# First block of a state-space and attention kernel: one exponential moved to ScalarE, key blocks placed elsewhere around the taps, input loads reordered

## The chip, the cores and the metric

The kernel runs on one NeuronCore of a Trainium2 chip. The metric is the device time of one execution in microseconds (us). The program is one launch made of several blocks that end in a barrier of all engines; the change touches the first of them only.

## The reference, cut to what matters

Two adaLN-like layers act on x (64 sequences of 32 tokens, 512 wide): a convolution along the feature axis with kernels that a state-space model gives, then a feed-forward layer with low-rank experts, then attention over a paged cache of keys and values, then a second feed-forward layer. The first block of the kernel computes the convolution, and beside it turns the cached keys for the attention.

```python
dt = jnp.exp(log_dt)
A = -jnp.exp(log_A_real) + 1j * A_imag
dtA = A * dt[:, None]
P = dtA[:, :, None] * jnp.arange(length, dtype=jnp.float32)
Cs = Cc * (jnp.exp(dtA) - 1.0) / A
K = 2.0 * jnp.einsum('hn,hnl->hl', Cs, jnp.exp(P)).real      # (32 heads, 512 taps)
...
k_f = jnp.fft.rfft(kernel, n=n); u_f = jnp.fft.rfft(u_m, n=n)
y = jnp.fft.irfft(u_f * k_f, n=n)[..., :Lq]                  # causal convolution per head
y = y + u_m * D[:, None]
return y * mask[:, None, :]
...
x = x + L0_ffn(L0_cond(x, ...), ...)
x = x + L1_ffn(L1_cond(x, ..., k_cache, v_cache, ...), ...)
```

## The kernel before

The first block is the function `prologue`. Its work, by engine:

- **VectorE** computes dt and A from 32-column tiles, then the angles (48 multiples of the imaginary part of dtA for each of 2048 modes, a 128x768 tile), brings them into the range of the sine (`reduce_angle`), then computes the magnitudes: `exp_exact` is an exponential out of 14 VectorE operations on the 128x768 tile (clamp, split off the power of two, a polynomial). It multiplies magnitude by sine and cosine (`er`, `ei`), works out the coefficients (sums of products in 128x16 tiles), and hands `ur`, `ui` over. Every operation waits for the one before it (class `Line`). Later it makes the masks, adds D to the taps, reduces the angles of the rotary embedding (128x1024 tiles), and then masks the result of each of the 32 heads (L312).
- **ScalarE** takes the sines of angles (L348), copies turned keys from PSUM to SBUF (`lay_out(n)`, L336, two operations for a block), copies half of the taps (L352), writes the taps to a DRAM scratch `taps` (L354), and reads them back as a Toeplitz tile for each head (`load(h)`, L342, tile `s_toe`, six buffers). These six buffers mean that head h+6 is loaded when head h is through.
- **TensorE** turns blocks of cached keys by transposes (`turn(n)`, L378: eight 128x128 transposes for a block, 16 blocks in all), computes the taps (L390: 128 small matmuls), and then convolves: four matmuls for each of the 32 heads (L399), which read the reversed input `um` and `s_toe`.
- **SyncE** loads the small inputs and the key blocks (`k_in`, four buffers, 512 KB a block), stores the turned blocks (`k_t`, L203), and loads the first feed-forward layer's weights after the store of block 12. The block can end only when all 16 stores have landed (L210).
- **GpSimd** multiplies the rotary tables; it isn't late for anything in this block.

Three things set the order of the key blocks. `EARLY = 9` blocks are turned before the taps. The others follow a head each: `late(h)` gives block 9 after head 3, block 10 after head 7, and so on to block 15 after head 27. And block n+4 is loaded when the copies of block n are done.

There are two DMA queues in use here: SyncE's (queue 1 in the profile) and ScalarE's (queue 10). Before the change the four loads of `um`, 1 MB each, stand in ScalarE's queue.

Of the kernel before, what the change touches and what calls it, by code (L numbers as in the profile page):

```python
# [19 lines left out]
ALU = mybir.AluOpType  # L20
ACT = mybir.ActivationFunctionType
AX = mybir.AxisListType

P = 128
# [29 lines left out]
NMUL = 48  # L54
# [46 lines left out]
def spread(ap, axis, n):  # L101

    ap = ap.unsqueeze(axis)
    shape = list(ap.shape)
    shape[axis] = n
    return ap.to_broadcast(shape)
# [35 lines left out]
def prologue(nc, ps, dram, taps, cst, um, mrow, k_t, y_t, cos, sin, ta, tb, inputs):  # L142
# [6 lines left out]

    TB, YB, EARLY, H = 4, 4, 9, D // 2  # L150
    TOE = 6
    with ExitStack() as ctx:
# [29 lines left out]
        flat = lambda x: x.rearrange("p a b -> p (a b)")  # L182
        late = lambda h: EARLY + h // 4 if h % 4 == 3 and EARLY + h // 4 < KT else None

        with nc.Block() as block:
            @block.sync
            def _(e):
                src = bass.AP(tensor=dram["L0_cond_log_dt"].tensor, offset=0, ap=[[0, P], [1, S]])
                e.dma_start(log_dt[:, :], src).then_inc(s_dt, 16)
                e.dma_start(raw[:, 1, :], dram["log_a"]).then_inc(s_dt, 16)  # L190
                e.dma_start(ai[:, :], dram["a_imag"]).then_inc(s_in, 16)
                e.dma_start(cc[:, :, :], dram["c"]).then_inc(s_in, 16)
                e.dma_start(dvec[:, :], dram["L0_cond_D"].rearrange("(o h) -> o h", o=1)).then_inc(s_in, 16)

                def load(n):
                    e.dma_start(k_in[:, n % TB, :], dram["k_cache"][n * P:(n + 1) * P, :]).then_inc(s_ki[n % TB], 16)

                for n in range(TB):
                    load(n)
                k_rows = k_t.rearrange("(t n d) x -> t d n x", n=PPT, d=P)  # L200
                for n in range(KT):
# [26 lines left out]
            def _(e):  # L228
# [18 lines left out]
                mulb = spread(mul, 1, HP)  # L247
                e.wait_ge(s_cst, 16)
                v(lambda e: e.tensor_tensor(ang[:, :, :], spread(dai, 2, NMUL), mulb, ALU.mult))
                reduce_angle(v, flat(ang[:, :, :]), flat(t1[:, :, :]), flat(sn[:, :, :]), flat(cs[:, :, :]))  # L250
                done["angles"] = line.n
                v(lambda e: e.tensor_tensor(ang[:, :, :], spread(dar, 2, NMUL), mulb, ALU.mult))
                exp_exact(v, flat(ang[:, :, :]), flat(mag[:, :, :]), flat(t1[:, :, :]), flat(t2[:, :, :]), flat(t3[:, :, :]))
                e.wait_ge(s_sin, 2)
                v(lambda e: e.tensor_tensor(er[:, :, :], mag[:, :, :], cs[:, :, :], ALU.mult))
                v(lambda e: e.tensor_tensor(ei[:, :, :], mag[:, :, :], sn[:, :, :], ALU.mult))

                zr, zi, nr, ni, x, u = w[3], ei[:, :, 1], w[4], w[5], w[6], w[7]
                cr, ci = cc[:, :, 0], cc[:, :, 1]
# [6 lines left out]
                v(lambda e: e.tensor_tensor(ni, ni, x, ALU.add))  # L266
                sr, si, den = w[8], w[9], w[10]
                v(lambda e: e.tensor_tensor(sr, nr, ar, ALU.mult))
# [4 lines left out]
                v(lambda e: e.tensor_tensor(si, si, x, ALU.subtract))  # L273
                v(lambda e: e.tensor_tensor(den, ar, ar, ALU.mult))
                v(lambda e: e.tensor_tensor(x, ai[:, :], ai[:, :], ALU.mult))
                v(lambda e: e.tensor_tensor(den, den, x, ALU.add))
                v(lambda e: e.reciprocal(u, den))
                v(lambda e: e.scalar_tensor_tensor(out=sr, in0=sr, scalar=2.0, in1=u, op0=ALU.mult, op1=ALU.mult))
# [38 lines left out]
            def _(e):  # L317
# [4 lines left out]
                for kind, name in enumerate(("L1_cond_q_norm_w", "L1_cond_k_norm_w")):  # L322
                    row = bass.AP(tensor=dram[name].tensor, offset=0, ap=[[0, P], [1, D]])
                    e.dma_start(nw[:, kind, :], row).then_inc(s_len, 16)
                for k in range(KB):
                    e.dma_start(um[:, k, :, :], dram["x_rev"][k * P:(k + 1) * P, :, :]).then_inc(s_x, 16)
                e.wait_ge(s_v, done["zeros"])
# [12 lines left out]
                def load(h):  # L340
                    src = bass.AP(tensor=taps.tensor, offset=h * KPW + 1, ap=[[1, P], [1, L]])
                    e.dma_start(toe[:, h % TOE, :], src).then_inc(s_toe[h % TOE], 16)  # L342

                for n in range(2):
                    lay_out(n)
# [3 lines left out]
                for n in range(2, EARLY):  # L349
# [4 lines left out]
                e.dma_start(taps[:, P:KPW].rearrange("h (a b) -> a h b", b=32),  # L354
                            kev[:, :, :, :].rearrange("a i t b -> a (i t) b")).then_inc(s_out, 16)
                e.wait_ge(s_out, 32)
                for h in range(TOE):
                    load(h)
                e.wait_ge(s_v, done["rope"])
                for x in (sin, cos):  # L360
# [9 lines left out]
            def _(e):  # L370
# [15 lines left out]
                for i in range(HP):  # L386
                    for a, b, first in ((ur, er, True), (ui, ei, False)):
                        for half in range(2):
                            rows = slice(half * NS, (half + 1) * NS)
                            last = e.matmul(ps[0:16, half, i * 32:(i + 1) * 32], a[rows, i, :], b[rows, i, 0:32],  # L390
                                            start=first, stop=not first)
                            if i == HP - 1 and not first:
                                last.then_inc(s_k, 1)
                e.wait_ge(s_x, 16 * KB)
                for h in range(S):
# [1250 lines left out]
```

## Time and profile before

| | |
|---|---|
| median of 3 runs | 2441.7 us (2440.74 to 2443.94) |
| the profiled execution's own time | 2454.87 us |
| its span, first to last instruction | 2453.0 us |
| TensorE busy | 2400.6 us, 98% of the span |
| VectorE, ScalarE, GpSimd busy | 1878.4, 1310.2, 719.9 us |
| the first block | 0 to about 98.8 us of the span |

The profiled execution is 13.2 us longer than the median of the runs; it serves to find where time goes, and differences are what is carried from it to the runs. Busy shares are means over the whole span, and the first block is 4% of it, so the first block is read by its own timeline.

### The profile page before, as it was taken

To read this page: it belongs to the slowest core of one execution; us is meant where nothing else is said; L and a number is where in the kernel's file an instruction comes from. 1 tells how busy PE (TensorE), PEld (TensorE's weight loads), DVE (VectorE), ACT (ScalarE), POOL (GpSimd) and SP (SyncE) were. 2 spreads that over 40 slices of the span, in tenths; PEclk is the share of its full clock that TensorE was granted. 3 is DMA by queue.
4 is the path that set the end of the run, shared out by engine and by line. 5 is a ranking of instruction groups with operands and counts; after the bars stand their busy time and mean duration, and the time that the engine had idled before them with its cause. 6 is when DMAs were issued, how large, how long until landed. Compare 5 with 4: busy or idle time off the path is not lost. (4 is left out here: it accounts for less than half of the span.)

```text
span 2453.0 us, 53992 instructions
## 1 busy us (share of the span) xinstructions
PE 2400.6 (98%) x16104; PEld 2167.1 (88%) x16104; DVE 1878.4 (77%) x3317; ACT 1310.2 (53%) x3758; POOL 719.9 (29%) x712
## 2 busy tenths in 40 slices
PE   5999999999999999999999999999999999999999
PEld 4888777777777999999999999999999998888877
DVE  7559999999961887788778877788778876666653
ACT  2335555555543677677767776676667761111120
POOL 1206666666641122222222222222222213131100
PEclk9999999999999999999999999999999999999999
DMA  8732333333347688888888888888788879666622
GB/s 312 258 120 87 94 98 95 95 115 94 98 125 245 222 295 276 294 298 291 281 285 303 295 284 282 293 297 295 273 295 295 295 268 283 219 209 207 204 69 103
DMA packets 434117, 542.36 MB, mean 221 GB/s; under 512 B 36980, under 2 KB 350100, under 8 KB 429460
## 3 DMA queue, kind: packets, MB, share of 16 engines
q1 hardware_dynamic: 390724, 394.24, 48.7%
q0 software_dynamic: 36864, 134.23, 16.2%
q10 hardware_dynamic: 6480, 13.26, 1.5%
q8 instruction: 28, 0.46, 0.1%
q14 instruction: 21, 0.17, 0.0%
HBM read 440.59 MB, written 101.01 MB: 221 GB/s over the span
## 5 line engine op out<-in xcount | busy, mean ns | idle before, releaser
L1296 DVE CUSTOM_DVE_ANT_0 at_sm<-ps,at_mask 128x544 f32<-128x544 f32 x512 | 369.3, 721 | 256.2 <-PE ps L1209 247.7
L1242 PE MATMUL ps<-at_pt,at_v_raw 128*128 128x128 f32 x4096 | 540.9, 275 | 1.7 <-issue 1.7
L1242 PEld LDWEIGHTS ps<-at_pt,at_v_raw 128*128 128x128 f32 x4096 | 497.6, 192 | 1.9 <-issue 1.9
L1359 ACT ACTIVATE at_pt<-ps 128x512 f32<-128x512 f32 x512 | 303.9, 594 | 299.4 <-PE ps L1218 194.9
L942 POOL TENSOR_TENSOR pr_m<-pr_qn,tb 128x256 f32<-128x256 f32 x320 | 331.6, 1056 | 307.0 <-DVE pr_qn L911 291.8
L1372 ACT ACTIVATE at_pr<-at_sm,at_nm 128x544 f32<-128x544 f32 x512 | 383.1, 748 | 59.1 <-DVE at_nm L1296 54.9
L1289 DVE TENSOR_TENSOR at_k_lo<-shared,at_k_hi 128x1088 fp32r<-128x1088 f32 x256 | 325.9, 1273 | 0.0
L762 PE MATMUL ps<-pr_hi,xh 128*128 (+1 forms) x768 | 317.7, 414 | 6.1 <-DVE pr_qn L911 5.0
L1167 POOL DMA_INDIRECT at_v_raw<-v_cache,at_idx x256 | 276.9, 1082 | 113.9 <-issue 62.0
L1218 PE MATMUL ps<-constants,at_pr 128*128 128x128 f32 x2048 | 306.5, 272 | 0.0
L764 PE MATMUL ps<-pr_hi,xl 128*128 (+1 forms) x768 | 303.3, 395 | 0.0
L763 PE MATMUL ps<-pr_lo,xh 128*128 (+1 forms) x768 | 303.2, 395 | 0.0
L868 ACT ACTIVATE pr_sq<-ps 128x128 f32<-128x128 f32 x640 | 168.0, 277 | 229.7 <-DVE f_a L904 224.4
L1173 POOL COPY at_idx<-at_rows 128x4 uint32 (+1 forms) x64 | 11.8, 184 | 868.4 <-PE ps L1249 801.7
L1209 PE MATMUL ps<-at_k_hi,at_q_hi 128*128 128x272 f32 x1024 | 255.5, 330 | 3.1 <-issue 1.2
L1218 PEld LDWEIGHTS ps<-constants,at_pr 128*128 128x128 f32 x2048 | 243.5, 140 | 0.0
L1209 PE MATMUL ps<-at_k_hi,at_q_lo 128*128 128x272 f32 x1024 | 211.9, 288 | 0.0
L1209 PE MATMUL ps<-at_k_lo,at_q_hi 128*128 128x272 f32 x1024 | 211.2, 287 | 0.0
L1477 ACT ACTIVATE op_ohi<-o_raw 128x2048 fp32r<-128x2048 f32 x31 | 59.6, 1922 | 273.5 <-PE ps L1534 243.1
L1530 PE MATMUL ps<-op_ohi,op_wlo 128*128 128x512 f32 x512 | 201.2, 393 | 0.0
L1529 PE MATMUL ps<-op_ohi,op_whi 128*128 128x512 f32 x512 | 200.9, 392 | 0.0
L922 DVE TENSOR_TENSOR pr_m<-pr_qn,ta 128x512 f32<-128x512 f32 x160 | 195.9, 1224 | 0.0
(239 smaller groups left out, 4299.3 us busy)
## 6 DMA issues: line engine op xcount, KB each, us to landing
shared<-k_t SPq DMA_DIRECT2D x1024, 128.0 KB
qk_t<-pr_stage SPq DMA_DIRECT2D x160, 256.0 KB, 2.3
shared<-qk_t SPq DMA_DIRECT2D x64, 512.0 KB, 7.3
o_t<-at_ot SPq DMA_DIRECT2D x64, 512.0 KB
shared<-ri_d SPq DMA_DIRECT2D x32, 1024.0 KB, 8.3
o_raw<-o_t SPq DMA_DIRECT2D x32, 1024.0 KB, 6.1
f_w<-wqkv SPq DMA_DIRECT2D x12, 1024.0 KB, 5.9
s_k_in<-k_cache SPq DMA_DIRECT2D x16, 512.0 KB, 8.0
```

Source lines behind the costliest of these rows:

```text
L762: e.matmul(out, xh[:, k, cols], hi, start=(k == 0), stop=False)
L763: e.matmul(out, xh[:, k, cols], lo, start=False, stop=False)
L764: last = e.matmul(out, xl[:, k, cols], hi, start=False, stop=(k == KB - 1))
L942: ins = e.tensor_tensor(heads(m2[:, q, :])[:, :, a], heads(qn[:, q, :])[:, :, b], table(tb, i, j - 3, a), ALU.mult)
L1167: e.indirect_dma_start(out=v_raw[:, q, c, :], out_offset=None, in_=dram["v_cache"], in_offset=bass.IndirectOffsetOnAxis(ap=idx[:, q, c:c + ...
L1209: last = e.matmul(ps[:, 2 * r + h, 0:W], a[:, q, mine], b[:, w, g % 2, h * W:(h + 1) * W], start=first, stop=end)
L1218: last = e.transpose(ps_w(jj % 2)[:, c * P:(c + 1) * P], pr[:, w, k, c * P:(c + 1) * P], ident)
L1242: e.matmul(sums(w, k), v_raw[:, q, c, g * D:(g + 1) * D], pt[:, jj % 4, c * P:(c + 1) * P], start=(k == 0 and c == 0), stop=False, skip_gr ...
L1289: e.tensor_tensor(two(k_lo), raw, two(k_hi).bitcast(F32), ALU.subtract).then_inc(s_lo, 1)
L1296: e.tensor_tensor_reduce(out=halves(sm[:, r, :]), in0=ps[:, 2 * r:2 * r + 2, 0:W], in1=halves(mask[:, q, :]), scale=-SC, scalar=3e38, op0= ...
L1359: e.activation(pt[:, jj % 4, :], ps_w(jj % 2), ACT.Copy).then_inc(s_pt, 1)
L1372: e.activation(pr[:, w, k, :], sm[:, r, :], ACT.Exp, bias=nm[:, at], scale=-1.0, accum_out=su[:, at]).then_inc(s_e, 1)
```

## The change

The diff, with all that concerns the steps:

```diff
-    TB, YB, EARLY, H = 4, 4, 9, D // 2
+    TB, YB, EARLY, GAP, H = 4, 4, 5, 8, D // 2
...
-        late = lambda h: EARLY + h // 4 if h % 4 == 3 and EARLY + h // 4 < KT else None
+        late = lambda h: GAP + h // 4 if h % 4 == 1 and GAP + h // 4 < KT else None
...
                 e.dma_start(raw[:, 1, :], dram["log_a"]).then_inc(s_dt, 16)
+
+                def load(n):
+                    e.dma_start(k_in[:, n % TB, :], dram["k_cache"][n * P:(n + 1) * P, :]).then_inc(s_ki[n % TB], 16)
+
+                load(0)
                 e.dma_start(ai[:, :], dram["a_imag"]).then_inc(s_in, 16)
                 e.dma_start(cc[:, :, :], dram["c"]).then_inc(s_in, 16)
                 e.dma_start(dvec[:, :], dram["L0_cond_D"].rearrange("(o h) -> o h", o=1)).then_inc(s_in, 16)
...
-                for n in range(TB):
+                for n in range(1, TB):
                     load(n)
+                for k in range(KB):
+                    e.dma_start(um[:, k, :, :], dram["x_rev"][k * P:(k + 1) * P, :, :]).then_inc(s_x, 16)
...
                 e.wait_ge(s_cst, 16)
+                v(lambda e: e.tensor_tensor(t2[:, :, :], spread(dar, 2, NMUL), mulb, ALU.mult))
+                done["exponents"] = line.n
                 v(lambda e: e.tensor_tensor(ang[:, :, :], spread(dai, 2, NMUL), mulb, ALU.mult))
                 reduce_angle(v, flat(ang[:, :, :]), flat(t1[:, :, :]), flat(sn[:, :, :]), flat(cs[:, :, :]))
                 done["angles"] = line.n
-                v(lambda e: e.tensor_tensor(ang[:, :, :], spread(dar, 2, NMUL), mulb, ALU.mult))
-                exp_exact(v, flat(ang[:, :, :]), flat(mag[:, :, :]), flat(t1[:, :, :]), flat(t2[:, :, :]), flat(t3[:, :, :]))
-                e.wait_ge(s_sin, 2)
...
+                v(lambda e: e.tensor_tensor(den, ar, ar, ALU.mult))
+                v(lambda e: e.tensor_tensor(x, ai[:, :], ai[:, :], ALU.mult))
+                v(lambda e: e.tensor_tensor(den, den, x, ALU.add))
+                v(lambda e: e.reciprocal(u, den))
+                e.wait_ge(s_sin, 3)
...
-                for k in range(KB):
-                    e.dma_start(um[:, k, :, :], dram["x_rev"][k * P:(k + 1) * P, :, :]).then_inc(s_x, 16)
...
+                e.wait_ge(s_v, done["exponents"])
+                e.activation(mag[:, :, :], t2[:, :, :], ACT.Exp).then_inc(s_sin, 1)
                 for n in range(2):
                     lay_out(n)
...
                             kev[:, :, :, :].rearrange("a i t b -> a (i t) b")).then_inc(s_out, 16)
+                for n in range(EARLY, EARLY + 2):
+                    lay_out(n)
                 e.wait_ge(s_out, 32)
                 for h in range(TOE):
                     load(h)
+                for n in range(EARLY + 2, GAP):
+                    lay_out(n)
...
+                for n in range(EARLY, GAP):
+                    turn(n)
                 e.wait_ge(s_x, 16 * KB)
```

The four operations on `den` and `u` are the same as before and stand earlier. After it, blocks 0 to 4 are turned ahead of the taps, 5 to 7 between the taps and head 0, and 8 to 15 behind heads 1, 5, ..., 29.

On ScalarE, from its first DMA on, this stands in order before (L336 is the copy of turned keys, L348 the sines, L352 and L354 the taps, L361 the rotary sines):

```order
L328 DMA taps<-s_zeros 32x128
L336 ACT_TABLE_LOAD
L336 ACTIVATE s_k_out<-ps 128x4x4x32 x4
L348 ACT_TABLE_LOAD
L348 ACTIVATE s_sn<-s_sn 128x768
L348 ACTIVATE s_cs<-s_cs 128x768
L336 ACTIVATE s_k_out<-ps 128x4x4x32 x14
L352 ACTIVATE s_kev<-ps 16x16x32
L354 DMA taps<-s_kev 16x32x32
L342 DMA s_toe<-taps 128x512 x6
L361 ACTIVATE shared<-shared 128x1024 x2
```

And this now:

```order
L346 ACT_TABLE_LOAD
L346 ACTIVATE s_mag<-s_t 128x768
L337 ACTIVATE s_k_out<-ps 128x4x4x32 x4
L351 ACT_TABLE_LOAD
L351 ACTIVATE s_sn<-s_sn 128x768
L351 ACTIVATE s_cs<-s_cs 128x768
L337 ACTIVATE s_k_out<-ps 128x4x4x32 x6
L355 ACTIVATE s_kev<-ps 16x16x32
L357 DMA taps<-s_kev 16x32x32
L337 ACTIVATE s_k_out<-ps 128x4x4x32 x4
L343 DMA s_toe<-taps 128x512 x6
L337 ACTIVATE s_k_out<-ps 128x4x4x32 x2
```

The exponential (`s_mag`) stands first, the number of table loads in this stretch is two in both, and of the 14 copies that stood between the sines and the taps six are left; four stand between the write of the taps and the first reads, two behind these.

On SyncE's queue the start was this:

```order
L190 DMA s_raw<-log_a 128x16
L191 DMA s_ai<-a_imag 128x16
L192 DMA s_cc<-c 128x32
L193 DMA s_dvec<-L_cond_D 1x32
L196 DMA s_k_in<-k_cache 128x1024 x4
L203 DMA k_t<-s_k_out 128x4x256
```

And it is this now:

```order
L190 DMA s_raw<-log_a 128x16
L193 DMA s_k_in<-k_cache 128x1024
L196 DMA s_ai<-a_imag 128x16
L197 DMA s_cc<-c 128x32
L198 DMA s_dvec<-L_cond_D 1x32
L193 DMA s_k_in<-k_cache 128x1024 x3
L202 DMA um<-x_rev 128x2048 x4
L206 DMA k_t<-s_k_out 128x4x256
```

The first key block has passed three small inputs, and the 4 MB of `um` stand ahead of the first store and of key block 4.

On TensorE, the rows behind the last matmul of the taps (L397) are these now; before, the row of 24 transposes (three blocks) was part of the 72 at the start, and after head 0 came heads 1 to 3 before a block:

```order
L397 MATMUL ps<-s_ei,s_ui 16x32 x2
L385 MATMUL ps<-constants,s_k_in 128x128 x24
L408 MATMUL ps<-um,s_toe 128x256
L408 MATMUL ps<-um,s_toe 128x192
L408 MATMUL ps<-um,s_toe 128x128
L408 MATMUL ps<-um,s_toe 128x64
```

There is one key block more among the heads than before (eight instead of seven), and three between taps and heads.

## Rows read from the trace of the kernel before

**Rows 1.** The page: span, and busy time of each engine.
```profile
span 2453.0 us, 53992 instructions
PE 2400.6 (98%) x16104; PEld 2167.1 (88%) x16104; DVE 1878.4 (77%) x3317; ACT 1310.2 (53%) x3758; POOL 719.9 (29%) x712
```

**Rows 2.** Waits of 0 to 200 us: total, times, longest.
```profile
PE ps L399 <- DMA s_toe<-taps: 8.6, 1, 8.6
```

**Rows 3.** Timeline of VectorE in the first block: start, length (us), line, operation.
```profile
9.27 0.17 DVE L246 TENSOR_TENSOR s_small<-s_ai,s_ex 128x16 f32<-128x16 f32 x1
...
18.41 0.56 DVE L111 TENSOR_SCALAR s_ang<-s_ang 128x768 f32<-128x768 f32 x1
...
30.32 0.96 DVE L255 TENSOR_TENSOR s_er<-s_mag,s_cs 128x768 f32<-128x768 f32 x1
...
35.05 0.17 DVE L274 TENSOR_TENSOR s_small<-s_small 128x16 f32<-128x16 f32 x1
...
35.97 0.18 DVE L278 SCALAR_TENSOR_TENSOR s_small<-s_small 128x16 f32<-128x16 f32 x1
...
98.19 0.59 DVE L312 TENSOR_TENSOR shared<-ps,mrow 128x256 f32<-128x256 f32 x1 [0.60 <-PE ps L399]
```

**Rows 4.** Timeline of ScalarE (ACT) and its DMA queue (ACTq).
```profile
19.54 0.85 ACT L348 ACTIVATE s_sn<-s_sn 128x768 f32<-128x768 f32 x1
...
43.77 0.33 ACTq L354 DMA_DIRECT2D taps<-s_kev  x1
47.91 2.76 ACTq L342 DMA_DIRECT2D s_toe<-taps  x6
...
59.18 1.08 ACT L336 ACTIVATE s_k_out<-ps 128x512 f32<-128x512 f32 x2 [3.60 <-PE ps L378]
```

**Rows 5.** Timeline of TensorE; a row may merge many instructions.
```profile
33.97 1.97 PE L378 MATMUL ps<-constants,s_k_in 128*128 128x128 f32 x8 [0.74 <-DMA s_k_in<-k_cache]
...
39.17 0.29 PE L390 MATMUL ps<-s_er,s_ur 64*16 64x32 f32 x4
...
42.46 0.22 PE L390 MATMUL ps<-s_ei,s_ui 64*16 64x32 f32 x4
51.32 7.33 PE L399 MATMUL ps<-um,s_toe 128*128 128x256 f32 x32 [8.64 <-DMA s_toe<-taps]
...
92.32 1.04 PE L378 MATMUL ps<-constants,s_k_in 128*128 128x128 f32 x8
93.20 4.95 PE L399 MATMUL ps<-um,s_toe 128*128 128x256 f32 x32
99.10 1.49 PE L625 MATMUL ps<-shared,f_g 128*32 128x512 f32 x11 [0.95 <-PEq L185]
```

**Rows 6.** Stretches: busy time of each engine, granted clock, DMA share, GB/s.
```profile
0.00:40.00 40.00, 18.52 (x104) 14.95 (x106) 32.31 (x76) 14.67 (x22) 0.95 (x6) 1.00 0.91 352
46.00:56.00 10.00, 4.68 (x16) 4.36 (x17) 7.91 (x9) 2.00 (x2) 0.34 (x1) 0.50 0.63 187
60.00:80.00 20.00, 20.00 (x143) 19.28 (x142) 8.57 (x14) 3.52 (x7) 14.26 (x7) 1.00 0.99 340
80.00:99.00 19.00, 18.15 (x129) 17.34 (x127) 8.46 (x14) 3.25 (x6) 0.00 (x0) 1.00 0.93 321
```

**Rows 7.** DMA issues of 0 to 200 us: count, KB each, median us to landing.
```profile
s_k_in<-k_cache SPq DMA_DIRECT2D x16, 512.0 KB, 8.0
k_t<-s_k_out SPq DMA_DIRECT2D x16, 512.0 KB, 7.1
s_toe<-taps ACTq DMA_DIRECT2D x32, 256.0 KB, 5.5
um<-x_rev ACTq DMA_DIRECT2D x4, 1024.0 KB, 14.8
```

**Rows 8.** The same for block 13's store, issued at 82.86 us.
```profile
k_t<-s_k_out SPq DMA_DIRECT2D x1, 512.0 KB, 12.6
```

**Rows 9.** The same for block 15's store, issued at 94.1 us.
```profile
k_t<-s_k_out SPq DMA_DIRECT2D x1, 512.0 KB, 4.3
```

More of the change, by code:

```diff
@@ L193, in _ @@
                 e.dma_start(dvec[:, :], dram["L0_cond_D"].rearrange("(o h) -> o h", o=1)).then_inc(s_in, 16)
-                def load(n):
-                    e.dma_start(k_in[:, n % TB, :], dram["k_cache"][n * P:(n + 1) * P, :]).then_inc(s_ki[n % TB], 16)
-                for n in range(TB):
+                for n in range(1, TB):
                     load(n)
+                for k in range(KB):
+                    e.dma_start(um[:, k, :, :], dram["x_rev"][k * P:(k + 1) * P, :, :]).then_inc(s_x, 16)
                 k_rows = k_t.rearrange("(t n d) x -> t d n x", n=PPT, d=P)
@@ L251, in _ @@
                 done["angles"] = line.n
-                v(lambda e: e.tensor_tensor(ang[:, :, :], spread(dar, 2, NMUL), mulb, ALU.mult))
-                exp_exact(v, flat(ang[:, :, :]), flat(mag[:, :, :]), flat(t1[:, :, :]), flat(t2[:, :, :]), flat(t3[:, :, :]))
-                e.wait_ge(s_sin, 2)
+                zr, zi, nr, ni, x, u = w[3], ei[:, :, 1], w[4], w[5], w[6], w[7]
+                sr, si, den = w[8], w[9], w[10]
+                v(lambda e: e.tensor_tensor(den, ar, ar, ALU.mult))
[3 more added lines that the diff above has]
+                e.wait_ge(s_sin, 3)
                 v(lambda e: e.tensor_tensor(er[:, :, :], mag[:, :, :], cs[:, :, :], ALU.mult))
                 v(lambda e: e.tensor_tensor(ei[:, :, :], mag[:, :, :], sn[:, :, :], ALU.mult))
-                zr, zi, nr, ni, x, u = w[3], ei[:, :, 1], w[4], w[5], w[6], w[7]
                 cr, ci = cc[:, :, 0], cc[:, :, 1]
@@ L266, in _ @@
                 v(lambda e: e.tensor_tensor(ni, ni, x, ALU.add))
-                sr, si, den = w[8], w[9], w[10]
                 v(lambda e: e.tensor_tensor(sr, nr, ar, ALU.mult))
@@ L273, in _ @@
                 v(lambda e: e.tensor_tensor(si, si, x, ALU.subtract))
[L274 to L277, printed above, removed]
                 v(lambda e: e.scalar_tensor_tensor(out=sr, in0=sr, scalar=2.0, in1=u, op0=ALU.mult, op1=ALU.mult))
```

## The prediction

> **What bounds the kernel now.** The page comes first: TensorE is busy in 98% of the span [rows 1], so time can only be won where TensorE stands still or runs slowly, or where a whole block is shortened. All that is edited lies in the first block, which ends with VectorE's last mask at 98.19 + 0.59 = 98.8 us [rows 3]; TensorE starts the next block at 99.10 [rows 5]. I therefore read the first 100 us by timelines, engine by engine, and take the rest as moved in one piece: behind 99 us nothing is edited, and no engine there waits for something that is timed from the launch.
>
> The first block has two stages. Up to 51.3 us a chain runs: VectorE's angles and magnitudes, then `er` at 30.32, the coefficients, the taps on TensorE until 42.46 + 0.22 = 42.7 us, the write of the taps at 43.77, their reads from 47.91, head 0 at 51.32 [rows 3 to 5]. The one long wait of TensorE in it is the 8.6 us for the first Toeplitz tile [rows 2]. Until the taps are ready the key blocks only fill gaps. The second stage, 51.32 to 93.20 + 4.95 = 98.15 us, is TensorE's: 32 heads and seven key blocks back to back [rows 5].
>
> A third thing must be watched. The DMA engines move 352 GB/s on average over the first 40 us, and are at a share of 0.99 with 340 GB/s from 60 to 80 [rows 6]. Block 13's store took 12.6 us to land, with the feed-forward weights ahead of it [rows 8]. The block ends when the slowest of TensorE's and SyncE's strands ends, and the second is close: block 15's store landed at 94.1 + 4.3 = 98.4 [rows 9], 0.4 us before VectorE was done.
>
> **The change part by part.** *The exponential.* `exp_exact` held VectorE from 18.41 to 30.32, 11.9 us [rows 3]. Now `er` waits for the three ScalarE operations. The product of the exponents moves ahead of the angles, so the angles are ready at 18.4 instead of 17.4 (one 128x768 product is 0.96 long and starts 1.0 before the next). The two sines take 0.85 each less some overlap [rows 4]: 18.4 + 1.6 + 0.2 for the semaphore = 20.25. The exponential is the same shape, about 0.85, and lies under VectorE's angles; its cover is VectorE's angles, from about 10.5 (one product and its gap behind the 9.5 us at which they began [rows 3]) to 18.4. So `er` starts at 20.25 instead of 30.32: 10.1 us off. The four operations for the reciprocal took 35.97 - 35.05 = 0.9 us on the chain [rows 3]; now they run in the wait for the sines: 0.9 off. Sum: 11.0 us earlier at the taps, whose matmuls then start at 39.17 - 11.0 = 28.2 and end at 31.7 [rows 5].
>
> *Key block 0 ahead of three small inputs.* These come perhaps 1.5 us later, and VectorE uses the first of them at 9.27 [rows 3]. No row says how long they had been there. I take 0; the bound is 1.5 us late.
>
> *Blocks 5 to 8 leave the front, `um` goes to SyncE's queue.* TensorE needs five blocks before the taps, 2.0 us each [rows 5]. Block 4 is now behind three key blocks, 4 MB of `um` and one store in its queue: with the constants and itself 7.7 MB. At 352 GB/s, a mean that holds the slow start of the launch [rows 6], that is there at 22 us and turned at 24; TensorE is wanted at 28.2. So 0, with 4 us of slack.
>
> *Blocks 5 to 7 between taps and head 0.* They fill TensorE's 8.6 us hole. The taps are written at 43.77 - 11.0 = 32.8 and need 47.91 - 43.77 = 4.1 us, so ScalarE may read at 36.9. Before that it has four copies, 1.1 us a block [rows 4]; block 6 is turned by 31.7 + 4.0 = 35.7 at the slow pace and copied by 36.8: just in time. The first tile then needs 51.32 - 47.91 = 3.4 us if nothing is in its way. Before, SyncE's queue was idle then; now two or three pairs of a store and a load are in flight. The median landing over the block is 5.5 us [rows 7], so the surcharge lies between 0 and 2.1; I take 1.0. Head 0 starts at 36.9 + 3.4 + 1.0 = 41.3, **10.0 us earlier** (9.0 to 11.0).
>
> *The heads.* One more key block is 93.20 - 92.32 = **0.9 us more**. Before, the first four heads ran 7.33 against 4.95 us for the last four [rows 5]: the granted clock is 0.50 from 46 to 56 us, the 1.2 GHz level [rows 6]. It fell after TensorE had been still since 42.7. Now the last block is turned near 37 to 38 and TensorE is still for 3 to 4 us. So 0 to 2.4 us come back; I take the middle, **1.2 us less**. The last head ends at 41.3 + 46.8 + 0.9 - 1.2 = 87.8.
>
> A remark on that clock: the Trainium skill (TensorE: Matmul & The Clock Gate, part 1, the clock gate) says that the array's default is the throttled level, and that activity releases it. The page of the profile shows 1.00 over the first 40 us, yet eight transposes took 1.97 us there and 1.04 at 92 us; the durations side with the skill, so that the turns of the front run at the slow level in both kernels. By the granted clock alone blocks 5 to 7 would take half as long; head 0 would not come sooner, since the taps' 4.1 us end later than these.
>
> *The end of the block.* Block 15 was turned at 92.32, and its store landed at 98.4, 6.1 us later, with four heads (4.95 us) to cover it. Now only two heads, 2.5 us, stand behind it. The turn starts 0.9 + 2.5 = 3.4 us before the last head's end, at 84.4; the store lands at 90.5. The block ends there and not at 87.8 + 0.6 = 88.4: **2.1 us lost**.
>
> *The same end by DMA.* The block moves 16 x 0.52 MB in, the same out, 32 x 0.26 MB of Toeplitz tiles, 4.2 MB of `um` [rows 7], 0.4 of constants and 1.6 of weights: 31.4 MB. 14.1 are through at 40 us (352 GB/s); 17.3 more at 340 to 360 GB/s are 48 to 51 us: 88 to 91. Both ways agree, so DMA is no further loss, but it stands right behind.
>
> Sum: 98.8 becomes 90.5 to 90.6, a shift of 10.0 + 1.2 - 0.9 - 2.1 = 8.2. The profiled execution would be 2454.87 - 8.2 = 2446.7 (span 2444.8). The runs' median lies 13.2 under the profiled one; with it, **2441.7 - 8.2 = 2433.5 us**. A measurement tells about 0.2% (4.9 us) from nothing.
>
> **Rivals.** *A. The next block starts slowly.* TensorE would stand still from 87.8 to 90.9, 3 us. After 42.7 it was granted 1.00 for a while and 0.50 from 46 on. If DMA is the later strand (91) or the heads end early, the still time passes 3.3 us and the clock may fall. L625, 3.6 us at full pace, then takes 7.2: gain 4.7, 2437.0.
>
> *B. `um` holds up the taps.* Block 4 is turned after 28.2 if the 7.7 MB take more than 26.2 us, which is under 294 GB/s from the launch on. The Trainium skill (DMA: Bandwidth & Descriptors, Queues, rings and completion order) says that descriptors of one queue are taken in ring order; no load can pass `um` by it. At 259 GB/s the block lands at 29.7 and is turned at 31.7: 3.5 us late, gain 4.7, also 2437.0. For it: 352 GB/s is what two queues did together, and now nearly all is in one. Against it: even with its slow start the stretch was 20% above the limit.
>
> *C. All goes well.* No surcharge on the first tile, the clock stays up, and block 15 lands in 5.4: 1.0 + 1.2 + 0.7 more: gain 11.1, 2430.6.
>
> *D. The Toeplitz tiles starve: slower.* Six tiles are in flight, and head h+6 must land within about five heads and a block, 7.1 us. Landings had a median of 5.5. The stores and loads of blocks 5 to 11 now run beside them throughout. If landings went to 9.5 us, six heads would take 9.9, 1.65 each, 53 us for the 32 and with the key blocks 60 against 47: 13 lost, 8.2 + 0.3 won, 2446. It decides from a landing of about 8.6 on. For it speaks the share of 0.99 [rows 6]; against it, that 60 to 80 us were just such a stretch and TensorE was busy 20.00 of 20 us.
>
> *E. It doesn't shorten the chain*: ScalarE must copy blocks 0 and 1 before the sines. If key block 1 came only as late as before, the sines would stay at 19.54, only 1.1 us late; to cancel everything it would have to come 10 us later. Gain near 0 only with B in its worst form: 2441.
>
> **How the numbers follow.** Forecast (gain 6.5 to 10) 0.60; A 0.14; B 0.07; C 0.11; D 0.04; E 0.04. The range from C's 2430.6, with 0.6 to spare, to A's and B's 2437.0 with 0.5: 2430.0 to 2437.5. It holds the forecast's cases, and most of A, B and C. Faster by over 0.2% means a gain over 4.9: the forecast, C, and about half of A and B, and what scatters beyond: 0.85. Slower is D: 0.04. The same: 0.11.
>
> **What would show it.** In the profile after: `er` at 20 to 21 us; the taps' matmuls ended by 32; block 4's turn done before them and no wait of these on `k_in`; first read of the taps at 37, head 0 at 40.5 to 42; heads at 1.2 us each; last head's end at 86.5 to 89, the last `k_t` store landing 2 to 3 us behind it, and SyncE's wait for it as the one that ends last; the next block's TensorE at 91 with a granted clock of 1.00. It would be wrong if `er` waited for ScalarE, if TensorE waited for `s_toe` more than a few tenths after head 0, or if stores queued up and the block ended well behind 91.

## The result, and the profile after

The changed kernel took 2438.87 us (median of 20 runs, 2435.49 to 2442.88), the kernel before 2443.81 us (20 runs, 2440.74 to 2448.12). The ratio is 0.998, with a 95% interval of 0.9974 to 0.9986: 4.9 us faster (3.4 to 6.4), where 8.2 were forecast. The time lies 1.4 us above the forecast's range.

The page of the changed kernel: span, and busy time of each engine, which answers to [rows 1].

```profile
span 2436.9 us, 53979 instructions
PE 2386.3 (98%) x16104; PEld 2160.7 (89%) x16104; DVE 1876.4 (77%) x3303; ACT 1320.2 (54%) x3759; POOL 718.1 (29%) x712
```

The profiled execution of the kernel before, 2454.87 us, lies above all of its twenty runs here, that of the changed kernel, 2438.88, is one of its twenty. So I take it that the two profiles come from different chips, and chips differ: the kernel before had medians of 2443.8, 2460.9, 2455.4 and 2461.6 us on four of them. Therefore I compare the stages of the first block and not the spans. Profiles of the same kernel, two of the one before and three of the changed one, start the next block within 0.4 us of each other, and head 0 within 0.5 us (before) and 1.2 us (changed). The waits of 0 to 200 us, total, times, longest, beside [rows 2]:

```profile
PE ps L385 <- DMA s_k_in<-k_cache: 19.7, 3, 10.4
...
PE ps L408 <- DMA s_toe<-taps: 5.9, 1, 5.9
```

VectorE's timeline, beside [rows 3]:

```profile
6.67 0.37 DVE L240 COPY s_raw<-s_log_dt 64x16 f32<-64x16 f32 x2 [5.69 <-DMA s_raw<-log_a]
...
21.43 0.96 DVE L264 TENSOR_TENSOR s_er<-s_mag,s_cs 128x768 f32<-128x768 f32 x1 [0.80 <-ACT s_cs L351]
...
90.17 0.59 DVE L315 TENSOR_TENSOR shared<-ps,mrow 128x256 f32<-128x256 f32 x1 [0.60 <-PE ps L408]
```

`er` starts 8.9 us earlier than in [rows 3], and waits 0.8 us for the second sine, as forecast. But VectorE's first copy starts at 6.67, and before at 5.33: the whole chain begins 1.3 us late. ScalarE and its queue, beside [rows 4]:

```profile
34.04 0.33 ACTq L357 DMA_DIRECT2D taps<-s_kev  x1
34.47 2.06 ACT L337 ACTIVATE s_k_out<-ps 128x512 f32<-128x512 f32 x4 [0.86 <-PE ps L385]
37.03 3.37 ACTq L343 DMA_DIRECT2D s_toe<-taps  x6
```

TensorE, beside [rows 5]; 30 like rows of the taps' matmuls are left out:

```profile
26.25 1.97 PE L385 MATMUL ps<-constants,s_k_in 128*128 128x128 f32 x8 [10.43 <-DMA s_k_in<-k_cache]
29.36 0.29 PE L397 MATMUL ps<-s_er,s_ur 64*16 64x32 f32 x4 [1.14 <-DVE s_ui L291]
...
32.65 0.30 PE L397 MATMUL ps<-s_ei,s_ui 64*16 64x32 f32 x4
32.88 2.11 PE L385 MATMUL ps<-constants,s_k_in 128*128 128x128 f32 x16
35.71 1.06 PE L385 MATMUL ps<-constants,s_k_in 128*128 128x128 f32 x8 [0.71 <-ACT s_k_out L337]
42.64 4.66 PE L408 MATMUL ps<-um,s_toe 128*128 128x256 f32 x16 [5.87 <-DMA s_toe<-taps]
...
87.61 2.52 PE L408 MATMUL ps<-um,s_toe 128*128 128x256 f32 x16
91.98 3.64 PE L634 MATMUL ps<-shared,f_g 128*32 128x512 f32 x32 [1.85 <-PEq L185]
```

Head 0 starts at 42.64 (8.7 us earlier), the last head ends at 87.61 + 2.52 = 90.13, the next block starts at 91.98 (7.1 earlier). The 16 matmuls of heads 0 and 1 took 4.66 us, and those of heads 30 and 31 took 2.52. The stretches show why (busy time of PE, PEld, DVE, ACT, POOL, then the granted clock, the DMA share and GB/s), beside [rows 6]:

```profile
28.00:40.06 12.06, 6.92 (x154) 6.17 (x152) 10.01 (x21) 3.31 (x7) 0.00 (x0) 0.78 0.93 310
40.06:46.89 6.83, 4.25 (x14) 3.92 (x15) 4.22 (x6) 3.09 (x4) 0.95 (x1) 0.50 0.99 341
46.89:60.00 13.11, 13.11 (x96) 12.65 (x96) 5.52 (x9) 3.05 (x6) 13.11 (x7) 1.00 1.06 401
60.00:80.00 20.00, 20.00 (x143) 19.28 (x142) 8.51 (x15) 3.47 (x7) 4.53 (x2) 1.00 1.03 360
```

TensorE had been still since 35.71 + 1.06 = 36.8, and from 40.06 to 46.89 it was granted 0.50, 1.2 GHz, which covers heads 0 and 1 but for their last tenths. From 46.89 on it is never idle, at a DMA share of 1.03 to 1.06; no Toeplitz tile is late.

### The profile page after: what moved, and what is told of

Read it like the earlier page. It is cut to its first block and busy times, and to the rows that moved or that the text cites. A ratio compares the mean times of both kernels' runs of the same rounds, so it can differ in the third digit from the quotient of the medians.

```text
span 2436.9 us, 53979 instructions
## 1 busy us (share of the span) xinstructions
PE 2386.3 (98%) x16104; PEld 2160.7 (89%) x16104; DVE 1876.4 (77%) x3303; ACT 1320.2 (54%) x3759; POOL 718.1 (29%) x712
## 5 line engine op out<-in xcount | busy, mean ns | idle before, releaser
L1251 PE MATMUL ps<-at_pt,at_v_raw 128*128 128x128 f32 x4096 | 542.0, 276 | 1.7 <-issue 1.7
L1251 PEld LDWEIGHTS ps<-at_pt,at_v_raw 128*128 128x128 f32 x4096 | 498.6, 192 | 1.9 <-issue 1.9
L1295 DVE CAST at_k_hi<-shared 128x1088 fp32r<-128x1088 f32 x256 | 193.6, 756 | 3.4 <-DMA shared<-qk_t 3.0
```

What stands on the lines that cost most here:

```text
L1251: e.matmul(sums(w, k), v_raw[:, q, c, g * D:(g + 1) * D], pt[:, jj % 4, c * P:(c + 1) * P], start=(k == 0 and c == 0), stop=False, skip_gr ...
```

## Experiments

All ran on three other chips; each time is beside runs of the kernel before on its own chip. First the two kernels themselves again, on one chip. 

> The kernel before, unchanged, for a second profile of it. Theory 1 (the 12.3 us that its first profile had lost against the profile after between 805 and 2007 us, in the attention loop, are scatter of one execution): the stretch from the first score matmul to the first output projection matmul is within 3 us of the one after, about 1208 to 1212 us instead of 1220.5; ratio 1.000. Theory 2 (the change reaches into the attention): the stretch stays near 1220. The first block should end at 98.8 plus or minus 0.5 either way.

> The changed kernel, unchanged, for a second profile. If the late landing of log_a (6.67 instead of 5.33 us) is scatter of the launch, it comes at 5.3 to 5.7 here, and the next block's TensorE starts near 90.7 instead of 92.0; if the change causes it, both repeat within 0.3 us. If the fall of the clock at 797.8 us, which cost 1.5 us, belongs to the changed timing, it repeats; if it is a matter of phase it may not. Ratio to before 0.998.

Measured: before against itself 2460.53 against 2460.86, ratio 1.0 (0.9991 to 1.0009). Changed: 2451.18, ratio 0.9964 (0.9951 to 0.9976), 9.7 us. The stages of the block (us from the span's start; `er` and the starts of matmuls):

| | VectorE's first copy | er | taps | head 0 | last matmul of head 31 | next block |
|---|---|---|---|---|---|---|
| before, first profile | 5.33 | 30.32 | 39.17 | 51.32 | 97.87 | 99.10 |
| before_again | 5.31 | 30.35 | 39.20 | 50.84 | 97.11 | 98.68 |
| after, first profile | 6.67 | 21.43 | 29.36 | 42.64 | 89.85 | 91.98 |
| after_again | 5.67 | 20.52 | 28.44 | 41.73 | 89.63 | 91.76 |
| k0_behind | 5.07 | 19.82 | 27.85 | 43.35 | 91.45 | 93.57 |
| warm_gap | 5.91 | 20.67 | 28.59 | 42.48 | 87.76 | 89.89 |
| exp_alone | 5.84 | 20.60 | 37.66 | 49.99 | 96.31 | 97.53 |
| blocks_alone | 5.30 | 30.29 | 39.12 | 52.45 | 100.59 | 102.72 |
| gap_nine | 5.90 | 20.78 | 28.70 | 41.99 | 88.64 | 90.15 |
| quiet_reads | 5.74 | 20.50 | 28.43 | 39.93 | 87.24 | 90.81 |
| um_behind_act | 5.81 | 20.70 | 28.62 | 41.91 | 91.17 | 93.30 |
| gap_nine_warm | 5.52 | 20.27 | 28.19 | 43.66 | 89.53 | 90.82 |
| three_more_act | 5.81 | 20.66 | 28.58 | 41.87 | 90.03 | 92.77 |
| after_third | 5.78 | 20.67 | 28.59 | 42.92 | 89.45 | 91.57 |

What follows: the block's gain repeats (6.9 and 7.1 us). It is not 8.2, and the time that the runs gained is not the block's alone.

**Key block 0 behind the small inputs again (k0_behind).**

```diff
-                load(0)
                 e.dma_start(ai[:, :], dram["a_imag"]).then_inc(s_in, 16)
...
-                for n in range(1, TB):
+                for n in range(TB):
```

> The changed kernel with the load of key block 0 back behind the three small inputs. Theory 1 (that load disturbs the two inputs ahead of it or the launch): log_a lands at 5.3 us again, the taps' matmuls start 1.3 us earlier than 29.4, the time falls by about 1 us. Theory 2 (no influence): log_a lands as in the unchanged kernel of this call, the chain is the same within 0.3 us, and only the first turn is later, at no cost.

Measured: 2450.27, ratio 0.9957 (0.9944 to 0.997). VectorE's first copy, here and in after_again:

```profile
5.07 0.37 DVE L239 COPY s_raw<-s_log_dt 64x16 f32<-64x16 f32 x2 [4.09 <-DMA s_raw<-log_a]
```

```profile
5.67 0.38 DVE L240 COPY s_raw<-s_log_dt 64x16 f32<-64x16 f32 x2 [4.69 <-DMA s_raw<-log_a]
```

So the 512 KB load that stands *behind* `log_a` in the queue delays `log_a` itself: from issue to landing 4.0 us before and 5.4 in the changed kernel's first profile, 4.4 in after_again and 3.8 here. In all ten profiles with that load third in the queue the first copy starts at 5.52 to 6.67, in the four others at 5.07 to 5.33. The start of the chain was won back, but not the end: the write of the taps landed in 4.4 us instead of 3.0, head 0 started 6.5 us after the first read's issue instead of 5.6, TensorE waited 8.2 us for the first tile instead of 5.9, and the block ended 1.8 us later than after_again's. The DMA engines moved 367 GB/s between that issue and head 0, against 245 in after_again. But the changed kernel itself needed 6.3 us from issue to head 0 in after_third, so this one profile doesn't show that the edit made the end later.

**TensorE kept at work until head 0 (warm_gap).**

```diff
                 for n in range(EARLY, GAP):
                     turn(n)
+                for _ in range(44):
+                    e.transpose(ps[:, 3, 0:P], cst[:, C_ID:C_ID + P], cst[:, C_ID:C_ID + P])
                 e.wait_ge(s_x, 16 * KB)
```

> The changed kernel with 44 extra transposes of the identity between the last turn of the gap and head 0, written to a PSUM bank that head 3 overwrites; they add work that the reference doesn't need. Theory 1 (heads 0 and 1 took 4.5 instead of 2.4 us because the clock had fallen 3 us before head 0): the clock stays at 1.00 from the gap on, heads 0 and 1 take 2.4 us, the first block ends 2.1 us earlier, ratio lower by 0.0008. Rival (the first heads are held by the Toeplitz tiles): head 1 starts no sooner, the tiles' landings pace it, no change. If the extra work outlasts the wait, head 0 starts late by what is over, at most 1 us.

Measured: 2449.61, ratio 0.9957 (0.9944 to 0.9971). TensorE's timeline, and the stretch of 40 to 48 us:

```profile
35.84 4.97 PE L404 MATMUL ps<-constants 128*128 128x128 f32 x44
42.48 2.59 PE L410 MATMUL ps<-um,s_toe 128*128 128x256 f32 x16 [1.67 <-DMA s_toe<-taps]
...
89.89 3.64 PE L636 MATMUL ps<-shared,f_g 128*32 128x512 f32 x32 [1.85 <-PEq L185]
```

```profile
40.00:48.00 8.00, 6.33 (x47) 5.92 (x46) 4.78 (x7) 4.18 (x6) 2.83 (x2) 1.00 1.02 362
```

With work until 40.8 TensorE stands still for only 1.7 us, the clock stays at 1.00 and the first 16 matmuls take 2.59 us instead of 4.66. The heads' stage is 2.6 us shorter than after_again's, and the block ends 1.9 earlier. The clock's term is shown.

**The two halves apart (exp_alone, blocks_alone).** The first keeps the exponential and the new load order, with nine blocks ahead of the taps; the second is the kernel before with only the new places of the key blocks.

```diff
-    TB, YB, EARLY, GAP, H = 4, 4, 5, 8, D // 2
+    TB, YB, EARLY, GAP, H = 4, 4, 9, 9, D // 2
...
-        late = lambda h: GAP + h // 4 if h % 4 == 1 and GAP + h // 4 < KT else None
+        late = lambda h: GAP + h // 4 if h % 4 == 3 and GAP + h // 4 < KT else None
```

> The changed kernel with the key blocks where they were: nine turned before the taps, the others behind heads 3, 7, ..., 27. The exponential stays on ScalarE and the loads keep their new order. Theory 1 (the exponential is worth its 11 us only because the key blocks leave the front): key block 8 lands at 36 to 37 us as in both kernels, so its turn ends near 39 and the taps' matmuls start at 38.5 to 39.5 instead of 28.4; the first block ends within 1 us of 98.8, ratio 0.9995 to 1.000. Theory 2 (the chain on VectorE was the bound by itself): taps near 30, block end near 90.

> The kernel before with the new places of the key blocks alone; exponential on VectorE and loads as before. Theory 1: the taps' matmuls start at 39.2 as before, since VectorE bounds them (er at 30.3); the gap then holds three turns and their traffic, so head 0 starts at 51.5 to 53.5; the heads hold one key block more; the first block ends 1 to 3 us later, at 100 to 102. Theory 2 (each half brings its share): the block ends 3 us or more earlier than 98.8.

Measured: exp_alone 2451.08 against 2455.38, ratio 0.9983 (0.9973 to 0.9993), its block only 1.2 to 1.6 us shorter. blocks_alone 2457.86 (one run), its block 3.6 to 4.0 us *longer*. TensorE before the taps in exp_alone, then TensorE's two waits in blocks_alone:

```profile
35.77 1.97 PE L381 MATMUL ps<-constants,s_k_in 128*128 128x128 f32 x8 [0.63 <-DMA s_k_in<-k_cache]
```

```profile
PE ps L394 <- DVE s_ui L288: 10.3, 1, 10.3
PE ps L405 <- DMA s_toe<-taps: 5.9, 1, 5.9
```

Alone, the fast exponential finds TensorE busy with block 8 until 37.7, since its load landed at 35.7; alone, the five early blocks leave TensorE 10.3 us with nothing to do before taps that come no sooner. 1.2 to 1.6 won and 3.6 to 4.0 lost apart, 7 won together: one edit moves the bound off VectorE, the other off the loads.

**Four key blocks in the gap (gap_nine).**

```diff
-    TB, YB, EARLY, GAP, H = 4, 4, 5, 8, D // 2
+    TB, YB, EARLY, GAP, H = 4, 4, 5, 9, D // 2
...
-        late = lambda h: GAP + h // 4 if h % 4 == 1 and GAP + h // 4 < KT else None
+        late = lambda h: GAP + h // 4 if h % 4 == 3 and GAP + h // 4 < KT else None
```

> The changed kernel with four key blocks (5 to 8) between taps and head 0, and the others behind heads 3, 7, ..., 27. Theory (the last store's cover and the eighth block among the heads cost 0.9 us each): last head to next block 1.2 us instead of 2.1, 0.9 us less TensorE work among the heads, next block 1.8 us earlier, at about 90.0 if head 0 starts as in the changed kernel. Rival (a fourth pair of store and load beside the first Toeplitz reads): head 0 or the heads behind it come later by up to 1.5 us, and nothing is won.

Measured: 2440.50 (one run; before 2455.38). TensorE at head 0:

```profile
41.99 7.44 PE L408 MATMUL ps<-um,s_toe 128*128 128x256 f32 x32 [4.75 <-DMA s_toe<-taps]
```

Block end 90.15, 1.4 to 1.8 earlier than the changed kernel's: 0.9 by one block less among the heads, most of the rest since the last store now has four heads to cover it (the next block starts 1.5 us behind the last matmul's start instead of 2.1). The clock still fell at 40.2. Head 0 started 5.6 us after the first read's issue at 36.43, so the rival, a fourth pair of store and load under the first reads, cost nothing here. The block explains about 9 of the 14.9 us that this single run lies under the median before; the loop, read under um_behind_act, gives some 4 or 5 more; the rest is open.

**The first reads undisturbed (quiet_reads).**

```diff
+                    if n == EARLY:
+                        e.wait_ge(s_toe[0], 16)
```

This stands ahead of SyncE's store of block 5. 

> The changed kernel with SyncE waiting for the first Toeplitz tile before it stores block 5 (and so before all stores and loads behind it). Theory (the first read took 5.5 instead of 3.3 us because stores and loads of blocks 5, 6, 9 and 10 were in flight beside it): the first tile lands 3.3 to 3.8 us after its read is issued, the six within 4.5 us of each other, head 0 starts at 40.0 to 40.7. The clock may still be low, which costs heads 0 and 1 up to 2.1 us. The price is that the held traffic comes later; block 9's turn needs its load within about 8 us of head 0, which it has in 6 to 7. Rival (the read is slow because it must wait for the write of the taps or by itself): the first tile stays at 5 us or more.

Measured: 2443.12 (one run). TensorE at head 0 and at the block's end:

```profile
39.93 4.25 PE L410 MATMUL ps<-um,s_toe 128*128 128x256 f32 x16 [4.09 <-DMA s_toe<-taps]
...
90.81 2.54 PE L636 MATMUL ps<-shared,f_g 128*32 128x512 f32 x12 [3.29 <-PEq L185]
```

With SyncE's queue held, the reads that were issued at 36.37 start head 0 in 3.6 us; beside its stores and loads head 0 starts 5.6 us after the issue (42.64 - 37.03). The surcharge over the 3.4 of before is 2.2, the upper end of the forecast's bound and not the 1.0 taken. A page of the Trainium skill (DMA: Bandwidth & Descriptors, Queues, rings and completion order) says that "each SDMA engine round-robins between the queue rows it has work for"; by that rule a queue alone gets its tile sooner, and these two runs agree. Of the 1.8 us won at head 0 against after_again, half arrives: block 15's store took 4.3 us to land instead of 2.9, and TensorE stands still for 3.3 us at the end. That the traffic held back did this is likely, but not shown.

This run tells more of the clock than it was made for. TensorE stood still for 4.1 us only, about the 3 to 4 that the prediction had assumed, and the clock fell all the same: it was at 0.50 from head 0 on, and the first 16 matmuls took 4.25 us, 1.7 more than at full pace.

**um behind ScalarE's queue again, and ScalarE's count (um_behind_act, three_more_act).**

```diff
-                for k in range(KB):
-                    e.dma_start(um[:, k, :, :], dram["x_rev"][k * P:(k + 1) * P, :, :]).then_inc(s_x, 16)
...
+                for k in range(KB):
+                    e.dma_start(um[:, k, :, :], dram["x_rev"][k * P:(k + 1) * P, :, :]).then_inc(s_x, 16)
```

```diff
                 e.wait_ge(s_v, done["exponents"])
+                for i in range(3):
+                    e.activation(spare[:, i:i + 1], t2[:, 0, i:i + 1], ACT.Exp)
                 e.activation(mag[:, :, :], t2[:, :, :], ACT.Exp).then_inc(s_sin, 1)
```

> One edit to the changed kernel: the four loads of um stand in ScalarE's queue again, as before the change. Two questions. In the first block: rival B said that um in SyncE's queue could hold up block 4; the changed kernel's traces show no wait of the taps for it. With um on its own queue the share that SyncE's queue gets falls, so the key blocks come later, not earlier; I expect the taps' matmuls at 28 to 30 us, head 0 at 41 to 44, the next block at 91 to 94, so no gain. The attention loop: the kernels that had the old exponential and um in ScalarE's queue need 1220.5 to 1227 us from the first score matmul to the output projection, 2.5 to 3 us more than the others on the same chip, since every second iteration is 0.11 to 0.12 us longer, which begins with a ScalarE operation that starts 0.11 us later. Theory S (the length of ScalarE's instruction stream ahead of the loop decides: 417 instructions in the slower kernels, 414 in the others, 418 here): iterations alternate again or change in some other way. Rival V (VectorE's stream, 467 against 453, here 453): iterations are uniform, about 19.0 us each, and the loop is as long as the changed kernel's.

> One edit to the changed kernel: three exponentials of one column each into a spare tile ahead of the large exponential on ScalarE, which lie under VectorE's angles. They bring ScalarE's instructions ahead of the attention loop from 414 to 417, the count of the kernel before, and add 0.6 us at most to a ScalarE that has 7 us of slack there. First block: as the changed kernel's, within 0.5 us. Theory S (the place of ScalarE's loop in its instruction stream makes every second iteration 0.11 us longer): the alternation of the kernel before is back and the loop is 2.5 to 3 us longer. Rival V (it comes with VectorE's stream, or with something else in the old exponential): iterations stay uniform.

Measured: 2455.89 and 2452.35 (one run each; before 2461.63, after_third 2450.07). With `um` behind ScalarE's queue the block is 1.7 us longer than after_third's, partly by waits of heads for tiles (1.0 us in one), and the attention loop alternates again. In three_more_act the block is 0.8 to 1.2 us longer than in the three profiles of the changed kernel, where 0.5 was the bound set; the last store took 3.5 us instead of 2.9. TensorE around one iteration's start and the next one's in um_behind_act, and in after_third:

```profile
1155.10 1.06 PE L1258 MATMUL ps<-at_pt_new,at_v_new 128*128 128x128 f32 x8
...
1157.18 1.06 PE L1251 MATMUL ps<-at_pt,at_v_raw 128*128 128x128 f32 x8
1158.33 0.51 PE L1218 MATMUL ps<-at_k_hi,at_q_hi 128*128 128x272 f32 x2
...
1176.32 1.06 PE L1251 MATMUL ps<-at_pt,at_v_raw 128*128 128x128 f32 x8
1177.31 0.51 PE L1218 MATMUL ps<-at_k_hi,at_q_hi 128*128 128x272 f32 x2
```

```profile
1173.80 1.06 PE L1251 MATMUL ps<-at_pt,at_v_raw 128*128 128x128 f32 x8
1174.79 0.51 PE L1218 MATMUL ps<-at_k_hi,at_q_hi 128*128 128x272 f32 x2
```

At this one place of the iteration the next score matmul starts 0.99 us (at times 1.04) behind the start of the eight matmuls of L1251, and in every second iteration 1.15 where `um` stands in ScalarE's queue. Where the same pair follows directly elsewhere in the iteration it is 0.81 to 0.82 apart. Over 63 iterations the mean is 19.05 (before_again) and 19.04 (um_behind_act) against 18.98 to 18.99 in six kernels with `um` in SyncE's queue on the same two chips; on the third chip 18.98 (blocks_alone) against 18.90 to 18.91 in three. That is 3 to 5 us over the loop, won 700 us behind the last edited line. Theory S fell: with 417 instructions of ScalarE ahead of the loop, the number of the kernel before, three_more_act does not alternate. Rival V fell too, since um_behind_act has VectorE's new stream and alternates. What is shown is that the four loads in ScalarE's queue bring it back (iterations alternate by 0.1 to 0.17 us in all four profiles with them there, on each of the three chips and in the first profile before, and by at most 0.04 in the ten others); by which way is open.

**Both gains together (gap_nine_warm), beside the changed kernel (after_third).** The edits are gap_nine's and warm_gap's, with 28 transposes.

> Two edits to the changed kernel that each helped alone: four key blocks (5 to 8) between the taps and head 0 and the others behind heads 3, 7, ..., 27; and 28 transposes of the identity into a free PSUM bank behind these four, which keep TensorE busy until head 0. My theory of the miss says that they add up, since the one takes 0.9 us of key block out of the heads and 0.6 us off the end of the block, and the other takes out the 2.3 us that heads 0 and 1 lose at the granted clock of 0.50: head 0 at 41.5 to 43, the granted clock 1.00 from 33 us on, last head's last matmul at 86.5 to 87.5, the next block's TensorE at 88 to 89.5, that is 2.5 to 3.5 us earlier than the changed kernel's on this chip; ratio to the kernel before 0.9945 to 0.9960. Rival (DMA is the bound of the block, as the prediction's second sum had it, 88 to 91): the next block does not start before 90, whatever TensorE does, with SyncE's wait for the last store taking what the clock gives.

> The changed kernel again, beside the combination and on its chip, against the kernel before. By the stages its first block gives 6.9 to 7.1 us; the rest depends on whether the clock falls at the start of the attention (1.5 us) and on how long every second iteration of the loop is (0 to 3 us): ratio 0.996 to 0.998.

Measured: 2450.14, ratio 0.9958 (0.9945 to 0.9972), and 2450.07, ratio 0.9953 (0.9939 to 0.9966). No difference, where 2.5 to 3.5 us were expected. TensorE in the combination:

```profile
36.98 3.22 PE L404 MATMUL ps<-constants 128*128 128x128 f32 x28
43.66 4.53 PE L410 MATMUL ps<-um,s_toe 128*128 128x256 f32 x17 [3.46 <-DMA s_toe<-taps]
...
90.82 3.64 PE L636 MATMUL ps<-shared,f_g 128*32 128x512 f32 x32 [1.02 <-PEq L185]
```

The reads were issued at 36.31, but head 0 started 7.3 us later. The fourth key block's transfers lie under them, but they did so in gap_nine too, where it was 5.6; why it was 7.3 here is open. The transposes ended at 40.2, 3.5 us too early, and the clock fell at 43.75 after all. So the two gains were not tested together. The rival's number came, the next block started at 90.8 and not before 90, but not by its way: the last store, issued at 85.81, landed in 4.5 us, at 90.3, VectorE's last mask ended at 90.43, and the next block started 0.4 us later, as it starts 0.3 us behind the last mask before the change. TensorE's late heads ended this block, and whether DMA would bound it with the clock up stays untested. No kernel of this study got the next block to start before 89.89.

## Why the prediction was off

Of the 5.4 us between 2433.5 and 2438.87, 2.1 are the starting point: the median over three runs was 2441.7, over 20 it is 2443.81. The prediction took the 2441.7 as exact, and this alone carries the time out of the range: its upper end would be 2437.5 + 2.1 = 2439.6, and 2438.87 lies under that. The other 3.3 are gain that didn't come, 1.1 of it in the first block and 2.2 outside. Two steps failed there: the clock was to give back 1.2 us and gave 0.2, and the rest of the kernel was to move in one piece and did not. The 2446.7 for the profiled execution can't be compared, since the 13.2 us between profile and median were most likely a difference of chips. By the prediction's own steps:

- **The exponential, the reciprocal** (10.1 + 0.9 off): right. From VectorE's first copy to `er` 24.99 us became 14.76, 10.2 less, and the taps' matmuls came 0.9 more forward.
- **Key block 0 ahead of three small inputs** (0, bound 1.5): mis-sized, 1.3 us in the first profile, 0.4 to 0.6 in after_again. The bound held, by another way than argued: not the inputs behind the load were late, but `log_a` ahead of it.
- **Five blocks ahead of the taps** (0, 4 us of slack): right, but block 4 was turned at 28.2 and not at 24; the slack was 1.1 us. Rival B was nearer than its 0.07.
- **Head 0** (10.0 earlier, surcharge 1.0): 8.7 earlier. The write of the taps landed in 3.0 instead of 4.1 us, 1.1 won; the surcharge was 2.2, 1.2 lost. That these two cancel is luck. Blocks 5 to 7 were turned faster than the slow pace that was assumed (16 transposes in 2.11 us, 8 in 1.06), which brought head 0 no sooner, as the prediction's remark on the clock said.
- **The eighth block among the heads** (0.9 more): right; turn to head is 0.88.
- **The clock gives back 1.2 us** (0 to 2.4): this step failed. Heads 0 and 1 lost 4.66 - 2.52 = 2.1 us at 0.50, where before the first four lost 7.33 - 4.95 = 2.4 [rows 5]: 0.2 came back. In the two later profiles these heads lost 2.4 and 1.6 us. I had set the still time at 3 to 4 us and taken the middle of the two outcomes. The tile was late, so it was 5.9; but quiet_reads, with 4.1 us, lost 1.7 as well, so the assumed gap would have kept little more. The error was to count on half of the 2.4 coming back across any such gap. warm_gap shows both the cause and the size: with work in the gap all but 0.1 us of it came back.
- **The end of the block** (2.1 lost): 0.9 lost. Block 15's store landed in 2.9 us, not in 4.3; probably because the last Toeplitz reads, issued by 81.5, were over when it was issued at 88.5. (With four heads behind the last block, stores took 4.0 to 4.8 in five profiles.) Rival A's clock fall at the next block's start did not come in any of the three profiles of the changed kernel; it did in quiet_reads, where TensorE stood still for 3.3 us, and in three_more_act, after 2.5.

So the block gained 10.0 - 1.3 = 8.7 at head 0, lost 0.9 - 0.2 in the heads and 0.9 at the end: 7.1. It is near the forecast 8.2 partly by luck, since the end's term was 1.2 too dark and the clock's 1.0 too bright. The DMA check (88 to 91) is not what ended the block: in warm_gap TensorE's heads were shorter, and the 1.9 us that came of it arrived in full at the next block's start.

**Outside the block** the prediction took the rest as moved in one piece. That failed in both directions. The granted clock falls at the start of later stages or doesn't: at the first score matmuls it fell for 3.4 us in the first profile after (at 797.8), not in the first profile before. From the first score matmul to the first iteration took 19.0 to 19.4 us without a fall (three profiles), 20.9 to 22.2 with one of 3.4, and 23.0 to 23.6 with one of 6.8. At the last feed-forward layer it fell for 6.8 instead of 3.4 us, 1.2 us more. These two are 2.8 us, and 7.1 - 2.8 = 4.3 is within the interval measured; but these are two single executions, set beside medians of twenty, so the agreement is no proof. And before_again has the fall at the attention too, so this is the phase in which a stage meets the clock and not a cost of the change; whether the shift by 7 us makes it more frequent, these runs don't tell. The gain of the attention loop goes the other way: 7 of the block and 3 to 5 of the loop are about what two other chips gave, 9.7 and 11.6 us (on the third, exp_alone's 1.4 and 4.7 stand against 4.3 measured, 1.7 to 6.6). On the chip of the result the changed kernel isn't held at that place at all:

```profile
1174.44 1.06 PE L1251 MATMUL ps<-at_pt,at_v_raw 128*128 128x128 f32 x8
1175.33 1.06 PE L1258 MATMUL ps<-at_pt_new,at_v_new 128*128 128x128 f32 x8
...
1177.41 1.06 PE L1251 MATMUL ps<-at_pt,at_v_raw 128*128 128x128 f32 x8
1178.23 0.50 PE L1218 MATMUL ps<-at_k_hi,at_q_hi 128*128 128x272 f32 x2
```

The pair is 0.82 apart, and its iterations take 18.79 us. There may have been nothing to win there. No trace of the kernel before was taken on that chip, so this stays an argument.

## What to carry to other kernels

Before counting on a clock that stays up across a gap, look at every gap in the traces and what came of it: here it stayed up over one of 1.7 us and fell in those of 3.5, 4.1, 4.8 and 5.9, and the gap has to be worked out with its late transfer in it, from the last matmul to the first landed tile. A median of three runs is a term of the forecast with a width of its own: 2.1 us here, more than the range had to spare. A hole filled on one engine is filled with somebody's transfers too, and these lie under the very read that ends the hole: it started head 0 in 3.3 to 3.6 us without them, in 5.5 to 7.3 with them, and in 5.6 and 6.3 in two profiles of one kernel. And a small input at the head of a critical chain wants its queue empty behind it as well as ahead of it.

## What the hardware showed that was not expected

- A 512 KB load issued 0.5 us behind an 8 KB load, on the same queue, delayed the small one's landing: 3.8 to 4.0 us from issue became 4.2 to 5.4 (four profiles and ten). A 16 KB load ahead of both was later too, 3.9 to 4.3 instead of 3.5.
- The first of six 256 KB reads started head 0 3.3 to 3.6 us after its issue with the other queue still, and 5.5 to 7.3 with key blocks in flight.
- Four DMAs issued at launch by ScalarE instead of SyncE lengthened every second iteration of a loop that starts 700 us later by 0.1 to 0.16 us.
- The changed kernel's loop ran at 18.79 us an iteration on one chip and at 18.99 on two others, nearly all of it at one matmul that waits.
